# A pairwise-interaction tower on one core: two stages of 512 batch rows against four of 256, with three looked-up groups and a GpSimd clear behind every gather

## What is computed

```python
def reference(dense_ctx, ids, tbl_0, ..., tbl_31, W_top1, b_top1, W_top2, b_top2, W_top3, L0_rec_kernel):
    e = jnp.stack([tbl_0[ids[:, 0]], ..., tbl_31[ids[:, 31]]], axis=1)      # 1024 x 32 x 64
    p, q = e[:, ROW], e[:, COL]                                             # 496 pairs
    kp = jnp.einsum('bpj,ipj->bpi', p, L0_rec_kernel)
    z = jnp.sum(kp * q, axis=-1)                                            # 1024 x 496
    h = jnp.concatenate([z, dense_ctx], axis=1)
    h = jnp.maximum(h @ W_top1 + b_top1, 0.0)
    h = jnp.maximum(h @ W_top2 + b_top2, 0.0)
    return h @ W_top3
```

## Time and profile before

| | |
|---|---|
| three runs | 588.83 us median (588.6 to 599.1) |
| the profiled execution | 586.51 us |
| its span, first to last instruction | 584.7 us |
| outside the span | 1.8 us |
| mean granted TensorE clock | 0.912 |

### The profile page before, as it was taken

The page is one execution under the profiler, slowest core; times in us unless marked ns, Lnnn a source line. Parts: engine busy times, 40 slices in busy tenths (PEclk is TensorE's granted clock), DMA queues, the critical chain, the costliest instruction groups (busy, mean ns, idle before and its releaser), DMA issues.

```text
span 584.7 us, 5769 instructions
## 1 busy us (share of the span) xinstructions
PE 440.4 (75%) x2216; PEld 148.8 (25%) x2216; DVE 291.5 (50%) x250; ACT 59.9 (10%) x85; POOL 242.4 (41%) x260
## 2 busy tenths in 40 slices
PE   0105213858969998889885293799999999999998
PEld 0002001213323232223231031232323333333442
DVE  0001001536748677668661261576768788885000
ACT  0000100101010101000200110011001200020212
POOL 5777773545635551350667567166550000000000
PEclk9998655969989999899998588699999999999999
DMA  3112111112312222221311411011110000000000
GB/s 121 27 27 53 27 27 32 46 36 70 80 33 72 64 55 58 60 55 37 80 23 28 144 25 27 4 42 23 21 24 18 2 1 0 1 19 1 1 0 0
DMA packets 15404, 21.33 MB, mean 36 GB/s; under 512 B 5521, under 2 KB 5777, under 8 KB 15250
## 3 DMA queue, kind: packets, MB, share of 16 engines
q0 software_dynamic: 8192, 8.40, 7.7%
q1 hardware_dynamic: 6464, 11.80, 6.8%
q10 hardware_dynamic: 722, 0.76, 0.4%
HBM read 18.85 MB, written 0.00 MB: 32 GB/s over the span
## 4 chain that ended last, share of the span: by engine, by line
PE 65%; another core or an unknown queue 15%; issue 14%; DVE 5%; DVEq 0%; ACT 0%
PE kp L372 36%; PE z_ps L388 19%; DVE prod L344 5%; PE kp L409 5%; PE kp L414 2%; PE tr_ps L357 2%; PE kp L419 1%; DVEq L343 0%; ACT prod L312 0%; DVEq L342 0%; DVEq L340 0%
## 5 line engine op out<-in xcount | busy, mean ns | idle before, releaser
L344 DVE TENSOR_TENSOR prod<-kp,pair 128x1024 f32<-128x1024 f32 x248 | 290.1, 1219 | 242.7 <-remote 113.1
L255 POOL DMA_INDIRECT raw<-in_tbl,ids_sb x256 | 242.2, 946 | 194.2 <-PE tr_ps L357 92.2
L372 PE MATMUL kp<-pair,k_sb 64*128 64x512 f32 x992 | 253.9, 637 | 89.0 <-DVE prod L344 48.6
L372 PEld LDWEIGHTS kp<-pair,k_sb 64*128 64x128 f32 x992 | 87.7, 193 | 237.2 <-issue 134.4
L388 PE MATMUL z_ps<-prod,ones_sel 128*32 128x512 f32 x992 | 128.7, 640 | 0.0
L357 PE MATMUL tr_ps<-ident,raw 128*128 128x128 f32 x128 | 24.1, 318 | 52.9 <-DMA raw<-in_tbl,ids_sb 47.6
L270 ACT ACTIVATE pair<-tr_ps 128x512 f32<-128x512 f32 x32 | 19.1, 598 | 346.0 <-PE tr_ps L357 181.8
L388 PEld LDWEIGHTS z_ps<-prod,ones_sel 128*32 128x32 f32 x992 | 27.0, 114 | 91.4 <-issue 70.9
L357 PEld LDWEIGHTS tr_ps<-ident,raw 128*128 128x128 f32 x128 | 15.5, 157 | 77.6 <-issue 43.1
L409 PE MATMUL kp<-z_sb,w_sb 128*128 128x512 f32 x64 | 28.2, 596 | 0.0
L280 ACT ACTIVATE pair<-pair 64x1024 f32<-64x1024 f32 x16 | 16.9, 1055 | 0.4
(11 more groups left out here) (5 smaller groups left out, 1.0 us busy)
## 6 DMA issues: line engine op xcount, KB each, us to landing
k_sb<-in_kd SPq DMA_DIRECT2D x31, 256.0 KB, 2.6
raw<-in_tbl,ids_sb POOLq DMA_INDIRECT x256
pair<-pair SPq DMA_DIRECT2D x16, 128.0 KB
w_sb<-in_w SPq DMA_DIRECT2D x1, 1024.0 KB
z_sb<-in_dense ACTq DMA_DIRECT2D x2, 256.0 KB
w_sb<-in_w SPq DMA_DIRECT2D x1, 512.0 KB
ids_sb<-in_ids ACTq DMA_DIRECT2D x1, 128.0 KB, 3.4
ident<-in_ident ACTq DMA_DIRECT2D x1, 64.0 KB
```

What stands on the lines that cost most here:

```text
L255: nc.gpsimd.indirect_dma_start(raw[:, g % RAW_RING, b, n, :], None, tables[f], bass.IndirectOffsetOnAxis(ap=ids_sb[:, h, b, f:f + 1], axis=0),
L344: nc.vector.tensor_tensor(prod[:, slot % PROD_RING, :, :], kp[slot % KP_RING][:, :, :], factor, ALU.mult).then_inc(prod_done, 1)
L372: last = nc.tensor.matmul(kp[slot % KP_RING][:, q, :], k_sb[rows, s, :], pair[rows, h * GROUPS + owner // 2, :], start=True, stop=True)
```

## The change

The work is cut in another way, and GpSimd gets another instruction.

- Stages: four of 256 rows in place of two of 512. A gather still takes 128 rows of one field, so a group of one stage needs four. The ring `raw` holds 16 groups of a stage (64 gathers). `GATHER` is the order of the gathers, `EVENT` that of the transposes: one group at a time in stage 0, two in stages 1 to 3.
- Units: a unit is two slots of 256 columns, with the same 1024 columns for DVE as a slot before. There are 248 of them, 62 to a stage. A product matmul and a summing matmul have 256 columns, and there are twice as many. Sums come in batches of 5, 6 and 5 units, `prod` holds 12 units.
- Lookups: in stage 0 groups 0, 2 and 4 take fields whose tables have 1000 rows and aren't gathered. SP loads their tables and ids, DVE compares the ids with the row numbers (48 compares of 125x256) and so makes a 0/1 matrix, and PE multiplies the table by it (16 matmuls for a group). 52 gathers are left in stage 0, 64 in each other stage: 244.
- GpSimd: behind every gather a clear of a scratch tile `rest` (128 partitions, 64 columns, float32), and a wait until it is done before the next gather.
- `TRANSPOSE_AT` is a list of 40 places, `slot_order()` and the mixed tiles are ordered anew, the matrices come in loads of 8 slots, the layers' weights are loaded over `k_sb` in the last stage, the third layer does both halves side by side, and the first layer of both halves comes before the second.

Unit 222 is where the last two groups (gathers 237 to 244) are transposed. The core of the diff:

```diff
-RB = ROWS // P
+BLOCKS = BATCH // P
-BATCH_SLOTS = 4
-BATCHES = SLOTS // BATCH_SLOTS
-TILES_PER_BATCH = 2 * BATCH_SLOTS
+K_LOAD = 8
+K_AHEAD = 3
 KP_RING = 3
-PROD_RING = 2 * BATCH_SLOTS
-RAW_RING = 4
-MIX_RING = 2
-MIX_AT = HALVES * GROUPS
+PROD_RING = 12
 LAG = 4
+RAW_RING = 16
+REST = 64
+WIDTH = 256
+STAGES = (1, 2, 2, 2)
+BATCH_UNITS = (5, 6, 5)
...
     for k in range(2, GROUPS):
         for a in range(2 * (k // 2)):
             order.append(((2 * a, (k, None)), (2 * a + 1, (k, None))))
-        if k % 2 == 0 and k >= LAG:
-            inside((k - LAG) // 2)
-    for m in range((GROUPS - LAG) // 2, FOURS):
-        inside(m)
+        if k >= 5 and (k % 4 == 1 or k == GROUPS - 1):
+            m = 2 * ((k - 5) // 4) if k < GROUPS - 1 else FOURS - 2
+            order.append(((4 * m, (2 * m + 1, None)), (4 * m + 1, (0, m))))
+            order.append(((4 * m + 4, (0, m + 1)), (4 * m + 5, (2 * m + 3, None))))
+            if m % 4 == 2:
+                order.append(((4 * m - 6, (1, m - 2)), (4 * m - 1, (1, m - 1))))
+                order.append(((4 * m + 2, (1, m)), (4 * m + 7, (1, m + 1))))
...
+LOOKUP = (0, 2, 4)
+SMALL = 1000
+SMALL_P, SMALL_C = 125, 8
+HOT_UNITS = 2 * SMALL_C * WIDTH // (2 * ROWS)
+UNIT_SLOTS = ROWS // WIDTH
+UNIT = [(st, s) for st in range(len(STAGES)) for s in range(0, SLOTS, UNIT_SLOTS)]
+UNITS = len(UNIT)
+CHUNK_UNITS = CHUNK_TILES // (2 * UNIT_SLOTS)
...
+def gather_order():
+    gathers, events = [], []
+    for st, n in enumerate(STAGES):
+        for k in range(0, GROUPS, n):
+            first = len(gathers)
+            if st or k not in LOOKUP:
+                gathers += [(g, st) for g in range(k, k + n)]
+            events.append((st, k, n, range(first, len(gathers))))
+    return gathers, events
...
+TRANSPOSE_AT = [0, 0, 0, 1, 2, 4, 7, 10, 13, 17, 23, 25, 31, 36, 41, 47, 52, 57, 64, 69, 75, 85, 93, 98, 109, 114,
+                123, 128, 137, 144, 155, 160, 171, 176, 185, 190, 199, 206, 217, 222]
...
-        ids_sb = sb("ids_sb", [P, HALVES, RB, FIELDS], I32)
-        raw = sb("raw", [P, RAW_RING, RB, 2, EMBED])
-        pair = sb("pair", [P, MIX_AT + 2 * MIX_RING, ROWS])
+        ids_sb = sb("ids_sb", [P, BLOCKS, FIELDS], I32)
+        raw = sb("raw", [P, RAW_RING, 2, 2, EMBED])
+        pair = sb("pair", [P, PLACES, WIDTH])
         k_sb = sb("k_sb", [P, SLOTS, P])
         prod = sb("prod", [P, PROD_RING, 2, ROWS])
-        z_sb = sb("z_sb", [P, HALVES, FC, ROWS])
+        z_sb = sb("z_sb", [P, FC, BATCH])
+        w3_sb = sb("w3_sb", [P, N2, 32])
+        hot_ids_sb = sb("hot_ids_sb", [P, len(LOOKUP), 2, WIDTH], I32)
+        row_sb = sb("row_sb", [P, SMALL_C])
+        rest = sb("rest", [P, REST])
...
+        T_SLOTS = len(LOOKUP) * 2 * SMALL_C * EMBED // P
+        table_sb = k_sb[:, SLOTS - T_SLOTS:SLOTS, :].rearrange("p a n -> p (a n)").rearrange(
+            "p (i n c e) -> p i n c e", i=len(LOOKUP), n=2, c=SMALL_C)
+        def hot(i, n, c):
+            at = (SMALL_C * n + c) * WIDTH
+            return prod[0:SMALL_P, HOT_UNITS * i + at // (2 * ROWS), at // ROWS % 2, at % ROWS:at % ROWS + WIDTH]
...
-        MLP = [(1, 0, n) for n in range(N1)] + [(2, 0, n) for n in range(N2)]
-        MLP += [(1, 1, n) for n in range(N1)] + [(2, 1, n) for n in range(N2)] + [(3, 0, 0), (3, 1, 0)]
+        MLP = [(1, h, n) for h in range(HALVES) for n in range(N1)]
+        MLP += [(2, h, n) for h in range(HALVES) for n in range(N2)] + [(3, 0, 0)]
...
-            for j in range(3):
+            load_hot_ids(0)
+            sp.dma_start(row_sb[0:SMALL_P, :], row_no).then_inc(row_no_in, 16)
+            load_tables(0)
+            load_hot_ids(1)
+            load_tables(1)
+            load_k(0)
+            load_hot_ids(2)
+            load_tables(2)
+            for j in range(1, K_AHEAD):
                 load_k(j)
-            for slot in range(HALVES * SLOTS):
-                h = slot // SLOTS
-                for m in fours_at(slot):
-                    mix_across(h, m)
-                j = batch_of(slot)
...
+            for u in range(UNITS):
+                st, s = UNIT[u]
+                for m in fours_at(u):
+                    mix_across(st, m)
+                j = s // K_LOAD
+                if st == 0 and s % K_LOAD == 0 and j + K_AHEAD < len(K_LOADS):
+                    sp.wait_ge(kp_done, u + 1)
+                    load_k(j + K_AHEAD)
+                if st == LAST and s == W_SLOTS:
+                    sp.wait_ge(kp_done, u)
+                    sp.dma_start(w1_sb, w1).then_inc(weights_in, 16)
+                    sp.dma_start(w2_sb, w2).then_inc(weights_in, 16)
+                    sp.dma_start(w3_sb[:, :, :], w3).then_inc(weights_in, 16)
...
         @block.gpsimd
         def _(pool):
             pool.wait_ge(ids_in, 16)
-            for g in range(HALVES * GROUPS):
-                h, k = divmod(g, GROUPS)
-                if g >= RAW_RING:
-                    pool.wait_ge(transposed, g - RAW_RING + 1)
-                for n in range(2):
-                    for b in range(RB):
-                        f = 2 * k + n
+            for r, (g, b) in enumerate(GATHER):
+                if r >= RAW_RING and EVENT_OF[r - RAW_RING] != (EVENT_OF[r - RAW_RING - 1] if r > RAW_RING else None):
+                    pool.wait_ge(transposed, EVENT_OF[r - RAW_RING] + 1)
+                for i in range(2):
+                    for n in range(2):
+                        f = 2 * g + n
                         nc.gpsimd.indirect_dma_start(
-                            raw[:, g % RAW_RING, b, n, :], None, tables[f],
-                            bass.IndirectOffsetOnAxis(ap=ids_sb[:, h, b, f:f + 1], axis=0),
-                        ).then_inc(raw_in[g % RAW_RING], 16)
+                            raw[:, r % RAW_RING, i, n, :], None, tables[f],
+                            bass.IndirectOffsetOnAxis(ap=ids_sb[:, 2 * b + i, f:f + 1], axis=0),
+                        ).then_inc(raw_in[r % RAW_RING], 16)
+                        nc.gpsimd.memset(rest[:, :], 0.0).then_inc(rested, 1)
+                        pool.wait_ge(rested, 4 * r + 2 * i + n + 1)
...
+            def evacuate(e):
+                st, k, n, raws = EVENT[e]
+                if st >= 2 and k == 0:
+                    act.wait_ge(prod_done, unit_at(st - 1, 0))
+                act.wait_ge(transposed, e + 1)
+                nc.scalar.activation(pair[:, group_place(st, k):group_place(st, k) + n, :],
+                                     tr_ps[:, 0:n * WIDTH].rearrange("p (n w) -> p n w", n=n),
+                                     ACT.Copy).then_inc(evacuated, 1)
...
+            dve.wait_ge(row_no_in, 16)
+            for i in range(len(LOOKUP)):
+                dve.wait_ge(hot_ids_in[i], 16)
+                for c in range(SMALL_C):
+                    for n in range(2):
+                        nc.vector.tensor_scalar(hot(i, n, c), hot_ids_sb[0:SMALL_P, i, n, :],
+                                                row_sb[0:SMALL_P, c:c + 1], None,
+                                                ALU.is_equal).then_inc(hot_ready, 1)
...
+                lookup = lookup_of(e)
+                if lookup is not None:
+                    pe.wait_ge(table_in[lookup], 2 * 16)
+                    for c in range(SMALL_C):
+                        for i in range(2):
+                            pe.wait_ge(hot_ready, 2 * (SMALL_C * lookup + c) + i + 1)
+                            last = nc.tensor.matmul(tr_ps[64 * i:64 * i + 64, 0:WIDTH],
+                                                    table_sb[0:SMALL_P, lookup, i, c, :], hot(lookup, i, c),
+                                                    start=(c == 0), stop=(c == SMALL_C - 1), skip_group_check=True)
+                for r in raws:
+                    g, b = GATHER[r]
+                    pe.wait_ge(raw_in[r % RAW_RING], (r // RAW_RING + 1) * 4 * 16)
+                    for i in range(2):
+                        to = (g - k) * WIDTH + i * P
+                        last = nc.tensor.transpose(tr_ps[:, to:to + P],
+                                                   raw[:, r % RAW_RING, i, :, :].rearrange("p a n -> p (a n)"),
+                                                   ident[:, :])
...
-            def products(slot):
-                h, s = divmod(slot, SLOTS)
-                if h == 0 and s % BATCH_SLOTS == 0:
-                    pe.wait_ge(k_in[s // BATCH_SLOTS], 16)
-                if slot >= KP_RING:
-                    pe.wait_ge(prod_done, slot - KP_RING + 1)
-                for q in range(2):
-                    owner = SLOT[s][q][0]
-                    rows = slice(64 * (owner % 2), 64 * (owner % 2) + 64)
-                    pe.wait_ge(evacuated, h * GROUPS + owner // 2 + 1)
-                    last = nc.tensor.matmul(kp[slot % KP_RING][:, q, :], k_sb[rows, s, :],
-                                            pair[rows, h * GROUPS + owner // 2, :], start=True, stop=True)
+            def products(u):
+                st, s = UNIT[u]
```

(78 more changed lines are left out.)

359 lines of the change are left out of this document (183 added, 176 removed).

## The result

| | before | after |
|---|---|---|
| median of 4 runs | 593.97 us (588.6 to 600.62) | 625.2 us (622.16 to 626.77) |
| profiled execution, its span | 586.51, 584.7 | 622.16, 620.2 |
| mean granted clock | 0.912 | 0.884 |

The changed kernel is slower: ratio 1.061, interval 1.0545 to 1.0682. The forecast of 475 us and the range of 440 to 540 were both wrong.

A forecast was written before the change was run, and what follows sets the result against it. It took gathers, 1.57 us apart, to bound the changed kernel: landed at 388.5, transposes to 389.8, 26 units to 425.5, layers 45.2 to 470.7, then 2.3 and 1.8, giving 475 us; range 440 to 540.

The forecast's parts named there:

- early starvation: Kernel before, both halves: PE idle for lack of gathered groups, 197 us of the span beside 387 us of work.
- rival A: PE sets the end, the clear hidden in the existing gap between gathers, step 1.25 to 1.44: 444 us; chance 0.18.
- waits for the ring: GpSimd waiting for PE to free ring places, 92.2 us in the kernel before, would go, as the ring holds a stage.
- 387: Changed kernel's GpSimd: the last gather was to end at 386.9 us, with gathers 1.57 us apart.
- 86: Changed kernel's end: some 86 us from the last gather's landing to the end.
- 47.6 us: Kernel before: PE's transposes waiting for gathers to land, read as a link between PE's rate and GpSimd's.
- gather step: GpSimd, start to start of gathers: gather 0.95, delay 0.15, clear 0.17, release 0.30, together 1.57 us.
- turning point of 1.44: Gather step in us below which PE, not the gathers, would set the end, at 444 us.
- Short matmuls: PE's matmuls of 256 columns were to halve in time; units 10% longer would add 34 us, giving 478.
- Layers and compares: Final layers on PE, 45.2 us; DVE's 48 compares, 0.43 us each, 20.6 us before its first product.
- Rival B: Clears on GpSimd wait for the DVE operation in flight, step 2.07: 597 us, slower than before; chance 0.07.
- The slower side: Chance of the changed kernel being slower than before by over 2%: 0.07.

The follow-up runs named there:

- four_448: Changed kernel with a clear of 448 columns and its wait behind every fourth gather only: 448.68 us on the second kind of chip, 634.44 on the first.
- plain_loads: Changed kernel with no GpSimd work: SP fetches as many blocks of the same size by plain loads, without lookup by id; 458.26 us, ratio 0.761.
- no_clear: Changed kernel without the clear and the wait behind each gather: 637.17 us, ratio 1.056 to the kernel before.
- rest_by_four: Changed kernel with one clear of 1792 columns and its wait behind every fourth gather, none behind the others: 506.52 us, ratio 0.842 to the kernel before.
- each_448_2: Changed kernel with 448 columns in place of 64 in the clear behind every gather, on the first kind of chip: 513.21 us.

## Why the prediction was wrong

**The step that failed** is the reading of PE's idle time in the kernel before: "the other 197 us of the span are early starvation, in both halves, because the first groups of a half allow few slots and a group of 512 rows takes 10 us to fetch". On the second kind of chip the same program took 474 us, over 110 less, with the same groups; and on the first kind it gave back 78 us (587.8 to 509.9) when its groups came later, with a pause behind each four gathers. So more than half of the 197 us was no want of data: engines that had all they waited for executed nothing, or one instruction at a time, while GpSimd gathered. My sum had no term for that, and the change, which takes away GpSimd's waits and lets it gather 80 times without a stop, feeds it. From the rows: between 40 and 120 us the changed kernel executes 108 matmul records, which at the 446 in 40 us of four_448 is 9.7 us of work. 70 us are lost there. The profiled 622.2 are 178 above rival A's 444, so some 108 more go in the later runs of gathers. The 92.2 us of waits for the ring, which I let go, are 99.9 in the new trace for the same reason: PE frees the ring late. GpSimd is done at 449 us and not at 387, and the end is PE's, 171 us later, where I had 86.

The hint stood in the trace. I used the row of GpSimd's waits for PE, and left two beside it unexplained:

```profile
PEld kp L372 <- issue: 134.4, 262, 18.1
...
DVE prod L344 <- remote: 113.1, 24, 21.2
```

with the 11.35 us of the chain above. Lateness of a group the profile names by its DMA, as in the 47.6 us that I did use. The two longest belong together. PE's 18.1 end at 78.78, 0.06 us after the DVE product of 77.50 to 78.72, so PE was most likely waiting for that product, to get its bank back, and "issue" doesn't say it. DVE's 21.2, ahead of the same product, are the hint: ACT starts only at 66.20 to copy what PE has transposed by 56.9, its last copy ends at 68.4, and DVE begins 9 us later. In all that time only GpSimd works without a stop.

**The gather step**: forecast 1.57, bounds 1.35 to 1.83; measured 1.39. Clear and release were right one by one (0.17; 0.27 against 0.30), but the clear begins 0.01 us after the gather, not 0.15. By my own turning point of 1.44 that should have been rival A's world, 444 us, so a right step would have made the forecast worse, not better.

**Rival A** was right as a floor, and on the second kind of chip it was the time: four_448, with a mean step of 1.37, took 448.7, plain_loads 458 on the first kind. What I held against it, that nothing overlaps a gather, was beside the point: the clear and its wait cost 0.14 us of step, and that is little enough.

**Short matmuls** came out at 1.406 a unit against 1.372, 8 us in all. The Trainium skill (TensorEngine Tiling (Array Packing), Instruction Overhead) had put the price at an estimated 18 us; these rows give less than half of it.

**Layers and compares**: layers 44.9 us, forecast 45.2. A compare took 370 ns on average, forecast 430.

**Rival B**: the clears kept 168 ns beside DVE's products. The Trainium skill (GPSIMD Engine Reference, Specifications) had excluded it for operands like these, and the trace agrees (it does so for the products; for the compares see the last section). The slower side came true with a chance of 0.07 that was all given to this mechanism; the real one was not among the rivals.

**Slower than before, and why.** That both kernels starve is shown, and that the pause decides. Why the changed one loses more is argued only. It asks 4290 matmuls and as many weight loads where the kernel before asks 2216 each. If instructions come at so many a microsecond, that work costs twice as much in a starved stretch. Or its deeper ring is to blame, which allows a run of 80 gathers against 72. Against the ring speaks no_clear: there the longest run is of 68 gathers at 1.25 us, from 5.5 to 90.3 us, shorter than that of the kernel before, the later ones are of 4 or 8, and it is still 5.6% slower. That leaves the number of instructions as the better of the two; no run varied it alone.

**Left open.** What differs between the two kinds of chip, and by which path a gather delays PE's instructions; that they arrive late, and aren't executed late for another reason, is itself read only from batches in which nothing else is waited for. Four jobs and the runs of the result met the first kind, one job the second; whether it is the chip, its host or its software, no run tells. The record gives the chip the number 7 both in the second job, where the kernel before took 474 us, and in the fifth, where it took 601, so the number doesn't tell. The loading of instruction blocks from memory is an unlikely path. The page's row for that queue in the changed kernel:

```profile
q8 instruction: 34, 0.56, 0.4%
```

34 transfers of 16 KB in 0.4% of 16 engines' span, 620.2 x 16 x 0.004 = 39.7 us, are about 1.2 us each; were none of them hidden, that is 40 us, not 178, and between two of them lie some 250 of PE's 8580 instructions, while the delay sits ahead of each single one. plain_loads, which isn't starved, has the same 34 transfers. How long a block was waited for before its transfer began, the row doesn't say. The Trainium skill (Runtime: NRT & Kernel Launch, Instruction fetch mechanics) says that engines take instructions in such blocks of 16 KiB and that the cost is mostly hidden; the size agrees with the row, and no rule there gives an instruction every 1.40 us.

## What to carry to other kernels

Read the rows that name no releaser before you call an idle engine short of data: an idle time put down to "issue" or "remote" on engines whose inputs are there, at the same time as a long row of GpSimd gathers, can be a supply of instructions that fails, and here it was worse the closer the gathers followed one another. Look at what ends such a wait, too: the 18.1 us above had no releaser and ended with a DVE product. Count an engine's records in a stretch, not its busy share (32 records still showed as 44% busy). Try a pause between gathers early, since here a clear behind every fourth gather was worth 13% to the kernel before and, in rest_by_four against the changed kernel, about 19% (506.5 against 625.2 us, medians of different jobs), and run the kernel before beside it on every chip, because on a chip of the other kind the same pause cost the kernel before 7%.

## What the runs showed of the hardware that I had not expected

- Two kinds of chip, or of whatever goes with it. The same program took 588 to 604 us (the medians of five series) on one kind and 474 on the other; with pauses, 509.9 and 509.6.
- The supply of instructions under gathers on the first kind: one PE instruction per 1.40 us with gathers 1.25 apart, one per 0.70 with clears of 0.17 between, nearly full pace with clears of 0.49 behind each or of 1.61 behind each fourth (402 and 370 records from 60 to 100 us, against 458 in plain_loads). In starved batches of sums the starts mostly lie 0.70, 1.40 or 2.10 us apart, multiples of 0.70.
- The granted clock falls with the starvation: 0.62 from 40 to 80 and 0.50, the 1.2 GHz level, from 80 to 120 us, after PE had run almost empty; 1.00, the 2.4 GHz level, from 60 to 100 us in four_448, with PE full.
- A clear of 128 partitions takes 0.17 us for 64 columns and 1.61 for 1792: 0.83 ns a column.
- DVE's compares, which read int32 from SBUF and write float32, get slower by clears beside them, where the products from PSUM don't: 348 ns on average with no GpSimd work (plain_loads), 369 to 387 with gathers and short clears or none, 512 in each_448_2, 549 in rest_by_four. The long clears so cost DVE 8 to 10 us over its 48 compares. Gathers feel the compares as well: up to 0.99 us beside them in the changed kernel, 0.95 otherwise.
